# A macaron block on one Trainium2 core: the loops over its sixteen phases written out

## The reference

```python
x = x + 0.5 * ffn(layernorm(x))
x = x + attn(layernorm(x))
x = x + 0.5 * ffn(layernorm(x))

# ffn
scores = einsum('bqd,bkd->bkq', q, k) / sqrt(256)
attn = softmax(scores, axis=-1)          # over the queries
z = einsum('bkq,bkv->bqv', attn, v)      # heads joined again
z = l2_normalize(z @ Wo); z = l2_normalize(z @ Wff)
z = gelu(z)

# attn: no softmax, so it is linear in the keys and values
attn = einsum('bhik,bhjk->bhij', q, k)
out = einsum('bhik,bhkj->bhij', attn, v)
out = out @ w_o.T + b_o
```

## Time and profile before

| | us |
|---|---|
| median of 3 runs | 3069.32 |
| lowest and highest | 3068.89, 3074.65 |
| the profiled execution's own time | 3079.44 |
| its span, first to last instruction | 3077.6 |
| busy in it: DVE, PE, ACT, POOL | 2810.2, 2752.8, 2737.8, 899.5 |
| mean granted TensorE clock | 0.973 of full |

### The profile page before, as it was taken

The page is one execution under the profiler, slowest core; times in us unless marked ns, Lnnn a source line. Parts: engine busy times, 40 slices in busy tenths (PEclk is TensorE's granted clock), DMA queues, the critical chain, the costliest instruction groups (busy, mean ns, idle before and its releaser), DMA issues.

```text
span 3077.6 us, 96889 instructions
## 1 busy us (share of the span) xinstructions
PE 2752.8 (89%) x36160; PEld 1078.5 (35%) x36160; DVE 2810.2 (91%) x5659; ACT 2737.8 (89%) x5028; POOL 899.5 (29%) x1195
## 2 busy tenths in 40 slices
PE   5989998989989899898998988988988888898887
PEld 2323443434434334343343433333323333232323
DVE  4999999999999999999999998999999999899986
ACT  2999888988889888898888989898998989899897
POOL 3333213322133221332313332122332312233222
PEclk8999999999999999999999999999999999999999
DMA  8222342323423234232341323433223343322332
GB/s 221 53 48 60 57 98 40 68 49 56 98 38 63 55 56 98 37 62 57 56 98 36 61 59 70 85 70 63 50 59 69 70 85 64 67 48 61 72 70 56
DMA packets 155355, 206.63 MB, mean 67 GB/s; under 512 B 34530, under 2 KB 88290, under 8 KB 154723
## 3 DMA queue, kind: packets, MB, share of 16 engines
q1 hardware_dynamic: 154594, 199.37, 31.3%
q0 software_dynamic: 256, 0.52, 0.1%
HBM read 46.66 MB, written 25.17 MB: 23 GB/s over the span
## 4 chain that ended last, share of the span: by engine, by line
PE 36%; issue 20%; SPq 18%; DVE 11%; POOL 8%; ACT 4%; DMA 2%; DVEq 0%; POOLq 0%; ACTq 0%
SPq L374 18%; PE ring L833 12%; PE ring L770 11%; PE o_acc L847 10%; DVE exp_ring L656 9%; POOL kq_parts L365 2%; POOL kq_rest L361 2%; POOL kq_parts L363 2%; POOL kq_parts L359 2%; PE ring L892 1%; ACT exp_ring L580 1%; DMA kq_stack<-kq_parts 1%; POOL v_scaled L513 1%; ACT w_xn L592 1%; PE ring L869 1%
## 5 line engine op out<-in xcount | busy, mean ns | idle before, releaser
L580 ACT ACTIVATE exp_ring<-exp_ring,neg_max 128x1024 f32<-128x1024 f32 x2048 | 2344.7, 1146 | 271.3 <-DVE exp_ring L656 254.5
L656 DVE TENSOR_SCALAR_CACHE_REDUCE exp_ring<-ring 128x1024 f32<-128x1024 f32 x2048 | 2408.9, 1216 | 189.1 <-PE ring L833 184.5
L833 PE MATMUL ring<-kq_stack 128*32 128x512 bf16 x16384 | 1165.7, 387 | 201.2 <-DVE exp_ring L656 50.7
L847 PE MATMUL o_acc<-exp_ring,v_scaled 128*32 128x512 f32 x8224 | 1091.7, 607 | 59.1 <-POOL v_scaled L513 37.9
L833 PEld LDWEIGHTS ring<-kq_stack 128*32 128x32 bf16 x16384 | 401.9, 97 | 1147.2 <-issue 413.3
L513 POOL TENSOR_TENSOR v_scaled<-v_now,exp_rsums 128x64 f32<-128x64 f32 x513 | 155.2, 303 | 1790.1 <-DVE exp_rsums L671 1770.4
L580 ACT ACTIVATION_READ_ACCUMULATOR exp_ring<-exp_ring,neg_max 128x1 f32 x2048 | 381.9, 186 | 0.0
L847 PEld LDWEIGHTS o_acc<-exp_ring,v_scaled 128*32 128x32 f32 x8224 | 249.7, 112 | 293.8 <-POOL v_scaled L513 64.4
L770 PE MATMUL ring<-ffn_wo_wowff,o_T 128*32 128x256 f32 x4352 | 258.4, 380 | 4.2 <-DVE exp_ring L656 2.8
L770 PE MATMUL ring<-xn_T,ffn_wqkv 128*32 128x512 f32 x2112 | 257.8, 609 | 3.0 <-DVE exp_ring L656 1.9
L359 POOL TENSOR_TENSOR kq_parts<-kq_stage,zero 128x512 bf16<-128x512 f32 x130 | 143.0, 1100 | 225.7 <-ACT kq_stage L610 144.5
(11 more groups left out here) (102 smaller groups left out, 1283.0 us busy)
## 6 DMA issues: line engine op xcount, KB each, us to landing
kq_stack<-kq_parts SPq DMA_DIRECT2D x2072, 64.0 KB, 2.4
x_post<-x_slots SPq DMA_DIRECT2D x17, 1024.0 KB, 5.5
x_prep<-x_slots SPq DMA_DIRECT2D x16, 1024.0 KB, 8.3
x_slots<-x_post SPq DMA_DIRECT2D x8, 1024.0 KB, 6.1
out<-x_post SPq DMA_DIRECT2D x8, 1024.0 KB, 4.5
x_prep<-in_L_attn_x SPq DMA_DIRECT2D x1, 1024.0 KB, 6.0
exp_ring<-in_L_attn_w_qkv SPq DMA_DIRECT2D x1, 512.0 KB
kq_stack<-kq_parts POOLq DMA_DIRECT2D x8, 64.0 KB, 3.6
```

Of the source, the lines that this page charges most:

```text
L580: nc.scalar.activation(e, e, ACT.Exp, bias=negmax[:, i % NM:i % NM + 1], scale=-1.0, accum_out=sums[:, g % EG, c:c + 1]).then_inc(exp_done, 1)
L656: nc.vector.tensor_scalar(E[:, (g % EG) * HQ + c, :].rearrange("p (b n) -> p b n", b=NB), ps, -1.0, None, ALU.mult, ALU.min, accum_out=neg ...
L833: last = mm(ps[k:k + COLS, n, :], kq[:, 0, c, j * P + k:j * P + k + COLS], kq[:, 1, c, n * BANK:(n + 1) * BANK], start=True, stop=True)
L847: last = mm(O[32 * c:32 * c + 32, n, :], vsc[a][:, g % EG, c, :], E[:, (g % EG) * HQ + c, n * BANK:(n + 1) * BANK], start=(a == 0 and j == ...
```

## The change

Both hardware loops become Python loops, so that phases 1 to 15 stand one after the other in the program, as phase 0 did before. Every wait has a constant, every DMA a fixed address. The order of the work, its tiles, places and waits stay the same for each phase.

```diff
         def before(p, kind):
-            return p * PER[kind] + AHEAD.get(kind, 0) if not (isinstance(p, int) and p < 0) else 0
+            return p * PER[kind] + AHEAD.get(kind, 0) if p >= 0 else 0
...
             part(plain_body, 0, False)
-            with engine.Fori(1, LINEAR) as p:
+            for p in range(1, LINEAR):
                 part(linear_body, p, True)
-            with engine.Fori(LINEAR, PHASES) as p:
+            for p in range(LINEAR, PHASES):
                 part(plain_body, p, False)
...
-                if linear or isinstance(p, int):
+                if linear or p == 0:
                     sp.wait_ge(x_stored, START + p * 16)
...
-                sp.dma_start(xr[:], tokens(xs[0 if isinstance(p, int) else p - 1])).then_inc(xr_loaded, 16)
+                sp.dma_start(xr[:], tokens(xs[0 if p == 0 else p - 1])).then_inc(xr_loaded, 16)
...
             phase(0, False)
-            with sp.Fori(1, LINEAR) as p:
+            for p in range(1, LINEAR):
                 phase(p, True)
-            with sp.Fori(LINEAR, PHASES) as p:
+            for p in range(LINEAR, PHASES):
                 phase(p, False)
```

More of the change, by code:

```diff
@@ L309, in linear_before @@
         def linear_before(p, linear):
-            return p if linear or (isinstance(p, int) and p == 0) else LINEAR
+            return p if linear or p == 0 else LINEAR
         def index(step):
@@ L432, in phase @@
                 stack_quarter(sp, 3)
-                if isinstance(p, int):
+                if p == 0:
                     sp.wait_ge(x1_done, 2)
```

## The result

The changed kernel takes 3025.82 us, the median of 4 runs (3021.01 to 3031.72), against 3069.11 us (3067.11 to 3074.65) for the kernel before on the same chip. The ratio is 0.9856, with a 95% interval of 0.984 to 0.9871: 43.3 us or 1.4% faster. The prediction said 3045.7 us, 23.6 us faster. The direction held, and so did the wide range of 8 in 10 (3021 to 3062). The forecast's own range (3036 to 3057, given a chance of 0.65) missed, and the gain was nearly twice what was forecast; the result lies 4 us from rival 1. The profiled execution of after took 3021.01 us, 5 us under its median, while that of before lay 10 us above its own.

The account below looks back on a forecast made before the run. The prediction took idle time of VectorE and TensorE together, chiefly fetch stalls at loop jumps, as what could go. Linear -22.0 and plain -1.6 us gave -23.6: 3069.3 to 3045.7 us; own range 3036 to 3057, 8 in 10 3021 to 3062.

Parts of the forecast that it names:

- rival 1: Everything gained: every plain phase runs like phase 0, 177.0 us, for -47.5 us and 3022 us; chance 0.17.
- Linear phases: Phases 1 to 8 lose the stall at their end jumps, each taking 189.70 to 189.98 us: -22.0 us (-22.8 to -20.6).
- VectorE's hidden pause: VectorE also pauses at its own jump, hidden by TensorE's longer one; removed in the same change, so not the next bound.
- Register rows at 0: Register instructions in the loops cost nothing, since sequencers run ahead and VectorE paces tiles at 1.14 us: 0 us.
- nothing in the list that SyncE works off gets longer: Argument against a slower kernel through GpSimd's stack wait, an outcome of about 3087 us given a chance of 0.05.
- rival 2: No measurable change: plain phases pay back most of the linear gain, at 184 us each; 3064 to 3075 us, chance 0.10.
- Plain phases: Phases 9 to 15 gain almost nothing in sum, phases 10 to 14 taking 180.6 us each: -1.6 us for all seven.
- the give-back: Without the jump's stall, TensorE's wait for scaled values at tile 18 of plain phases returns; tiles 16 to 31 about 25.4 us.
- correction (b): First tile of a plain phase also needs quarter 0, whose DMAs land barely in time: 0.4 us added per phase.
- correction (a): From plain phase to plain phase the DMAs start sooner than before phase 9, half a us earlier: -1.0 us per phase.
- 2.2 us for each us of lateness: Cost in tiles 16 to 31 of GpSimd's split starting later relative to tile 16, sized from phases 0 and 9.
- the prediction's own sign: Check in the new profile: tiles 16 to 31 of plain phases staying at 20.8 to 23 us would disprove the predicted loss there.

Follow-up runs that it names:

- linear_only: Linear phases 1 to 8 written out on every engine, plain phases still in a hardware loop, against the kernel before: 3042.65 us, ratio 0.9914.
- hinted_loops: The kernel before with both hardware loops kept and one prefetch hint for the back jump at each loop body's head on each engine: 3059.91 us, 0.9968.
- pe_only: Only TensorE's list written out, the other engines keeping their loops, against the kernel before: 3053.36 us, ratio 0.9945.

## Why the prediction was right in sign and short in size

Each term against the mean of the two profiles of before and of after (us over the stretch):

| | before | after | measured | predicted |
|---|---|---|---|---|
| phases 1 to 8 | 1540.7 | 1520.6 | -20.1 | -22.0 |
| phase 9 | 182.9 | 176.5 | -6.4 | -2.1 |
| phases 10 to 14 | 900.5 | 877.2 | -23.3 | -1.7 |
| phase 15 to the end | 212.0 | 208.4 | -3.6 | +2.2 |
| total span | 3072.0 | 3018.9 | -53.1 | -23.6 |

The profiled executions lie further apart than the medians, which give 43.3; so the table tells the shares of the terms better than their sizes.

- **Linear phases: right in the mechanism, 2 us short.** -20.1 lies just outside the term's own bounds (-22.8 to -20.6). The step "would measure 189.70 without the stall at its end" came out as 190.1 on average, since successive phases take 189.45, 190.0 and 190.6 in turn; one phase was again too thin a pattern. `linear_only` and `hinted_loops` show that the jump is its whole cause.
- **VectorE's hidden pause: right that it is there.** `pe_only` shows it, about 2 us in the linear loop and 4.1 us at the end of phase 9; in the plain loop it is no shorter than TensorE's.
- **Register rows at 0: right for their execution, and incomplete.** `hinted_loops` keeps them in the linear phases at no cost. What I did not price was that a loop fetches more code at each jump than it executes, and that such fetches stand beside the long DMA issues of SyncE. That they cause them is not shown. The sentence "nothing in the list that SyncE works off gets longer" was true, but the same list gets shorter in time: 24.1 us for quarter 1 fell to 22.4 and 21.9. I had even put the 24.1 against the 23.4 of phase 9 in rival 2, as an argument for no gain, without asking where 0.7 us came from.
- **Plain phases: the mechanism was there, the term was mis-sized.** On average over phases 10 to 14 of two profiles each, tiles 0 to 15 and 112 to 127 became 6.0 us shorter, the middle 0.7, and tiles 16 to 31 2.0 longer: a third of the gain was paid back, where I had nearly all of it. My 180.6 us is 23.2 + 25.4 + 111.8 + 19.8 for tiles 0 to 15, 16 to 31, 32 to 111 and 112 to 127, and 0.4 for quarter 0. Measured, as the mean of both profiles, are 23.2 + 22.9 + 109.6 + 19.8, which is 175.4 unrounded. So 2.5 us are the give-back and 2.2 the middle of phase 9, which was chance, mostly of the clock. 0.4 is correction (b), for which nothing shows: the last interval before phases 10 and 11 is 1.14 and 1.18 us. The give-back failed at correction (a), in two ways. First, phase 9's 26.39 us held a stretch at half clock, worth about 1.7 us, which stood in its row (0.94 against phase 0's 1.00 in the earlier trace rows). I took it for lateness, so "2.2 us for each us of lateness" should have been 1.0, and each plain phase inherited the slow clock; in the ten phases 10 to 14 of after's two profiles one had it. That is 1.5 of the 2.5 us. Second, the split was to come half a us sooner than in phase 9, and it came about 2 us sooner, some 0.9 because SyncE starts 2.1 us ahead of the phase and not 1.27, and some 1.2 because its issues are quicker.
- **Rival 1** gave 3022 us and named what was measured more closely than the forecast did. By the prediction's own sign (tiles 16 to 31 at 20.8 to 23 us) their mean of 22.9 speaks for it. Its price, all plain phases like phase 0 at 177.0, was even too high. My argument against it was one phase of one execution, taken as a law.

The choice between phase 0 and phase 9 as a pattern decided 24 us, and I made it without a second look at whether phase 9's blocks outside the disputed tiles resembled those of other plain phases. They did not: 111.84 against 109.5 to 110.6 in phases 10 to 14 of the same trace. That the result fell within 3021 to 3062 is owed to the width that rival 1 gave the range, not to the sum.

## What to carry to other kernels

Where a far jump closes a hardware loop, price it on every engine apart: the longest pause counts, taking away one engine's alone shows the next, and a prefetch hint at the head of the body removed nearly all of it at the taken jumps here, but cost some 5 us where the loop was left. Read the granted clock of a block before its time is put down to a wait. A stall that goes gives back only what was really bought with it, so measure the floor of the later stretch with no wait in it before booking a loss there. Before one phase is made the pattern for seven, compare its undisturbed blocks with those of its neighbours.

## What I had not expected of the hardware

- A far jump back costs TensorE 3.55 us (linear loop) or 4.88 us (plain loop) in the median, VectorE about 2 us of idle time in the linear loop and 4.1 us at the end of phase 9 (`pe_only`), GpSimd and SyncE, whose bodies are short, 0.2 to 0.3 us from branch to next row. With the hint TensorE's are 0.45 and 0.36 us.
- Instruction packets are 16 KB for TensorE and 8 KB for the others. Every issue of SyncE over 1 us, 157 of 157 in before and 130 of 130 in after, has one beside it, nearly always a 16 KB one, and their number roughly follows these.
- Behind the jumps of the plain loop TensorE was granted half clock for 2 to 10 us within the first 16 tiles (before, phases 10 to 15, first profile); in the straight kernel never there.
- 1 MB more of straight code on ScalarE (16384 instructions of 64 bytes, by (2.03 - 0.98) MB on the page) cost no time that four executions can tell.
